# A recurrent layer on one core: q normalised channel-major by two broadcast rows instead of token-major per chunk

## The reference

```python
q = hidden_states @ Wq
k = hidden_states @ Wk
v = hidden_states @ Wv
beta = jax.nn.sigmoid(hidden_states @ Wb + bb)
q = silu(causal_dwconv(q, qconv_w, qconv_b))      # 4 taps along the tokens
k = silu(causal_dwconv(k, kconv_w, kconv_b))
q = layernorm(q.reshape(Bs, Ls, H, DK), qn_w, qn_b)   # over the 128 channels of a head
k = layernorm(k.reshape(Bs, Ls, H, DK), kn_w, kn_b)
...
def step(S, inp):
    q_t, k_t, v_t, b_t = inp
    b = b_t[..., None, None]
    S = (1.0 - b) * S + b * (v_t[..., :, None] * k_t[..., None, :])
    o_t = jnp.einsum('bhvk,bhk->bhv', S, q_t)
```

## Time and profile before

| what | before |
|---|---|
| median of 3 runs (lowest, highest) | 2654.92 us (2653.37, 2655.7) |
| profiled execution, its own time | 2649.24 us |
| its span, first to last instruction | 2647.5 us |
| busy share of the span: PE / PEld / DVE / ACT / POOL | 96% / 85% / 67% / 42% / 32% |
| mean granted TensorE clock, share of full speed | 0.987 |

### The profile page before, as it was taken

The page is one execution under the profiler, slowest core; times in us unless marked ns, Lnnn a source line. Parts: engine busy times, 40 slices in busy tenths (PEclk is TensorE's granted clock), DMA queues, the critical chain, the costliest instruction groups (busy, mean ns, idle before and its releaser), DMA issues. The chain is left out here.

```text
span 2647.5 us, 44202 instructions
## 1 busy us (share of the span) xinstructions
PE 2538.9 (96%) x15744; PEld 2254.0 (85%) x15744; DVE 1779.9 (67%) x3716; ACT 1122.9 (42%) x1513; POOL 849.7 (32%) x442
## 2 busy tenths in 40 slices
PE   5899999999999999999999999997899999999997
PEld 4789889999999989999998999997788887888886
DVE  5678888888888888888888888888431222433232
ACT  5444454444444444444444444444432323322221
POOL 1245445443434334343434334344100000211220
PEclk8999999999999999999999999999999999999998
DMA  7544443643333353333354333342461101441320
GB/s 273 167 136 153 151 135 128 219 133 104 119 119 119 111 176 125 119 127 104 118 169 134 119 108 122 119 128 80 156 230 49 63 32 56 128 150 48 111 84 27
DMA packets 220876, 327.51 MB, mean 124 GB/s; under 512 B 56310, under 2 KB 156918, under 8 KB 216058
## 3 DMA queue, kind: packets, MB, share of 16 engines
q1 hardware_dynamic: 125946, 192.21, 22.2%
q10 hardware_dynamic: 86144, 109.06, 12.4%
q0 software_dynamic: 8704, 25.19, 3.1%
HBM read 237.77 MB, written 97.03 MB: 126 GB/s over the span
## 5 line engine op out<-in xcount | busy, mean ns | idle before, releaser
L983 DVE SCALAR_TENSOR_TENSOR xn_rows<-ps_proj,conv,xn_rows 128x1021 f32<-128x1021 f32 x381 | 488.0, 1281 | 127.8 <-ACT xn_rows L890 118.7
L1160 PE MATMUL ps_proj<-xt_hi,w_hi 128*128 128x512 f32 x1008 | 411.7, 408 | 20.1 <-DVE xn_rows L983 13.6
L1162 PE MATMUL ps_proj<-xt_hi,w_lo 128*128 128x512 f32 x1008 | 396.8, 394 | 0.0
L1161 PE MATMUL ps_proj<-xt_lo,w_hi 128*128 128x512 f32 x1008 | 395.4, 392 | 0.0
L941 ACT ACTIVATE rc_tok_k<-rc_tok_k,rc_small 128x128 f32<-128x128 f32 x512 | 204.2, 481 | 353.2 <-DVE rc_small L1017 353.2
L782 POOL TENSOR_TENSOR rc_k_state<-rc_tok_k,k_norm_rows 128x1024 f32<-128x1024 f32 x64 | 153.5, 2399 | 515.1 <-issue 397.5
L1182 PE MATMUL ps_proj<-wv_hi,xt_hi 128*128 128x256 f32 x1024 | 294.9, 288 | 0.6 <-PEq L75 0.6
L1183 PE MATMUL ps_proj<-wv_lo,xt_hi 128*128 128x256 f32 x1024 | 289.5, 283 | 0.0
L1184 PE MATMUL ps_proj<-wv_hi,xt_lo 128*128 128x256 f32 x1024 | 289.3, 283 | 0.0
L814 POOL TENSOR_TENSOR rc_small<-rc_small,rc_minus_half 128x16 f32<-128x16 f32 x64 | 187.2, 2924 | 218.9 <-DVE rc_small L1012 218.9
L890 ACT ACTIVATE xn_rows<-ps_proj,conv 128x1024 f32<-128x1024 f32 x127 | 152.9, 1204 | 231.7 <-PE rc_ps_work L1136 231.7
(11 more groups left out here) (177 smaller groups left out, 5770.9 us busy)
## 6 DMA issues: line engine op xcount, KB each, us to landing
rc_decay_all<-scratch_decay ACTq DMA_DIRECT2D x64, 512.0 KB, 3.5
rc_cum_all<-scratch_cum ACTq DMA_DIRECT2D x64, 512.0 KB, 3.6
scratch_o<-rc_o_sb ACTq DMA_DIRECT2D x64, 512.0 KB, 3.2
w_hi<-scratch_w_split SPq DMA_DIRECT2D x48, 512.0 KB, 4.0
w_lo<-scratch_w_split SPq DMA_DIRECT2D x48, 512.0 KB, 4.8
wv_hi<-scratch_wv_split SPq DMA_DIRECT2D x24, 512.0 KB, 3.9
wv_lo<-scratch_wv_split SPq DMA_DIRECT2D x24, 512.0 KB, 4.8
scratch_w_split<-w_hi SPq DMA_DIRECT2D x16, 512.0 KB, 2.8
```

Source lines behind the costliest of these rows:

```text
L983: nc.vector.scalar_tensor_tensor(out=act_cm[j][:, back:], in0=projected[:, 0:L - back], scalar=conv[par][:, j, t:t + 1], in1=act_cm[j][:, ...
L1160: nc.tensor.matmul(out, hi, xt_hi[:, k, cols], start=k == 0, stop=False)
L1161: nc.tensor.matmul(out, hi, xt_lo[:, k, cols], start=False, stop=False)
L1162: last = nc.tensor.matmul(out, lo, xt_hi[:, k, cols], start=False, stop=k == KC - 1)
```

## The change

**q's way.** The turned q is not copied out of PSUM any more and not turned back. ACT writes silu of q into a tile of its own (`q_silu`, two buffers). PE turns it only for its statistics, which DVE now takes straight from PSUM (`statistics(0)` reads `work(QT)`). The reciprocal standard deviation and the shift go into one small tile `rstd_shift` (128 tokens of a chunk as partitions; for q 16 columns: 8 chunks of rstd, 8 of shift). After the projection of v PE turns these 16 columns in one product into a 16 x 128 block of PSUM. ACT copies the block to `q_row_parts` and stores it to DRAM as 16 pieces of 512 bytes (`store_rows`), which lie there as two rows of 1024 values. Then, behind the normalising of k, ACT issues a load of the two rows to all 128 partitions (`load_rows`, `q_rows`, 128 x 2048 f32). In the next step DVE multiplies the channel-major q by the first row and adds the second, in place (`scale_q`: two tensor-tensor instructions of 128 x 1024, right behind the scan), and ACT reads that tile for `q_cm`.

**What goes with it.** On ACT `store_rows` stands before the normalising of k and waits for PE's product; `load_rows` stands behind it, before the eviction of the outputs. On DVE `normalise` and its 8 instructions are gone, and `statistics(0)` stands before `convolve(0)`. The turn of q before the projection of k is one instead of two. `ps_work` has six uses a step, so the waits on it are others: the turn of k waits until the statistics of q have read PSUM, the turn back of k until the outputs of the head before have been evicted. POOL's power waits for the product of the head before. `w_raw` and `wv_raw` now lie in tiles that the later stages use. A few semaphores are merged in `stage_tokens` and in the ranking, with the same order as before.

```diff
@@ pool
-                    nc.gpsimd.tensor_tensor(small[:, 6], small[:, 5], minus_half[:], ALU.pow
+                    after_step(pool, "q_rows_turned", B_.i - 1)
+                    nc.gpsimd.tensor_tensor(rstd_shift[:, :, 0], small[:, 5], minus_half[:], ALU.pow
                                             ).then_inc(S["rstd_done"], 1)
@@ act
-                def tokens(j):
...
+                def store_rows():
+
+                    after_step(act, "q_rows_turned", B_.i)
+                    after_step(act, "q_rows_stored", B_.i - 1, 16)
+                    nc.scalar.activation(q_row_parts[:], work(SC)[0:2 * NC, 0:P], ACT.Copy
+                                         ).then_inc(S["q_rows_copied"], 1)
+                    after_step(act, "q_rows_copied", B_.i)
+                    act.dma_start(row(scratch["q_rows"], B_.i).rearrange("(m p) -> m p", p=P), q_row_parts[:]
+                                  ).then_inc(S["q_rows_stored"], 16)
+
+                def load_rows():
+
+                    after_step(act, "q_rows_stored", B_.i, 16)
+                    after_step(act, "q_scaled", B_.i - 1, 2)
+                    act.dma_start(q_rows[:].rearrange("p k t -> p (k t)"),
+                                  row(scratch["q_rows"], B_.i).partition_broadcast(P)
+                                  ).then_inc(S["q_rows_loaded"], 16)
...
                 if C_.live:
-                    ready(0, "q_back", "q_ready", q_cm[C_.par])
+                    ready(0, "q_scaled", 2, q_silu[C_.par][:], "q_ready", q_cm[C_.par])
                 if B_.live:
                     load_decay(B_.par, B_.i, B_.pair)
-                    tokens(0)
...
                 if B_.live:
-
+                    store_rows()
                     after_step(act, "rstd_done", B_.i)
                     after_step(act, "shift_done", B_.i)
                     for c in range(NC):
...
                     last.then_inc(S["k_normed"], 1)
+                    load_rows()
@@ dve
-                def normalise():
-                    after_step(dve, "shift_done", B_.i)
-                    for c in range(NC):
-                        last = nc.vector.tensor_scalar(tok[0][:, c], tok[0][:, c], small[:, 6, 0, c:c + 1],
-                                                       small[:, 7, 0, c:c + 1], ALU.mult, ALU.add)
-                    last.then_inc(S["q_normed"], 1)
+                def scale_q():
+
+                    after_step(dve, "q_rows_loaded", C_.i, 16)
+                    after_step(dve, "q_turned", C_.i)
+                    nc.vector.tensor_tensor(q_silu[C_.par][:], q_silu[C_.par][:], q_rows[:, 0], ALU.mult
+                                            ).then_inc(S["q_scaled"], 1)
+                    after_step(dve, "q_scaled", C_.i, 2, 1)
+                    nc.vector.tensor_tensor(q_silu[C_.par][:], q_silu[C_.par][:], q_rows[:, 1], ALU.add
+                                            ).then_inc(S["q_scaled"], 1)
...
                                                  ALU.mult, ALU.add).then_inc(S["dmat_done"], 1)
+                    scale_q()
+                if B_.live:
+                    statistics(0)
                 if A_.live and not first_done(A_.i):
                     convolve(0)
                 if B_.live:
-                    statistics(0)
                     statistics(1)
...
-                if B_.live:
-                    normalise()
@@ pe
-                if C_.live:
-                    after_step(pe, "q_normed", C_.i)
-                    after_step(pe, "scores_done", D_.i - 1)
-                    turn(work(par, QB), lambda c: tok[0][:, c]).then_inc(S["q_back"], 1)
...
                 if B_.live:
                     after_step(pe, "k_silu", B_.i)
-                    after_step(pe, "q_tok", B_.i)
-                    turn(work(par, KT), lambda c: act_cm[1][:, c * P:(c + 1) * P]).then_inc(S["k_turned"], 1)
+                    after_step(pe, "stats_done", B_.i, 2, 1)
+                    turn(work(KT), lambda c: act_cm[1][:, c * P:(c + 1) * P]).then_inc(S["k_turned"], 1)
...
+                if B_.live:
+
+                    after_step(pe, "rstd_done", B_.i)
+                    after_step(pe, "shift_done", B_.i)
+                    if D_.live:
+                        after_step(pe, "scores_done", D_.i)
+                    nc.tensor.transpose(work(SC)[0:2 * NC, 0:P], rstd_shift[:, 0].rearrange("p k c -> p (k c)"),
+                                        ident[:]).then_inc(S["q_rows_turned"], 1)
                 if D_.live:
 
                     after_step(pe, "states_done", D_.i, NC - 1)
```

More of the change, by code:

```diff
@@ L538, in stage_recurrence @@
         act_cm = [keep["xn_rows"][:].rearrange("p t d -> p (t d)")[:, j * L:(j + 1) * L] for j in range(2)]
-        tok = [sb("tok_q", [P, NC, P]), sb("tok_k", [P, NC, P])]
+        tok_k = sb("tok_k", [P, NC, P])
+        q_silu = two("q_silu", [P, L])
+        q_rows = sb("q_rows", [P, 2, L])
         q_cm = two("q_cm", [P, L])
@@ L595, in stage_recurrence @@
         VC = NC // 2
-        QB, QT, KB, KT, UP, SC, OUT = range(7)
+        QT, KB, KT, UP, SC, OUT = range(6)
         class At:
@@ L879, in ready @@
                         after_step(act, "q_cum_done", C_.i - 2)
-                    nc.scalar.activation(out[:], work(par, (QB, KB)[j]), ACT.Identity,
+                    nc.scalar.activation(out[:], source, ACT.Identity,
                                          bias=norm[:, j, 1:2], scale=norm[:, j, 0:1]).then_inc(S[name_out], 1)
@@ L904, in silu @@
                     after_step(act, n + "_conv", B_.i, PAD)
-                    nc.scalar.activation(act_cm[j], act_cm[j], ACT.Silu).then_inc(S[n + "_silu"], 1)
+                    if j == 0:
+                        after_step(act, "q_turned", B_.i - 2)
+                        after_step(act, "q_ready", B_.i - 2)
+                    nc.scalar.activation((q_silu[B_.par][:], act_cm[1])[j], act_cm[j], ACT.Silu
+                                         ).then_inc(S[n + "_silu"], 1)
                 if B_.live:
@@ L1766, in build @@
             keep["beta_steps"] = first_stages.enter_context(nc.sbuf_tensor("beta_steps", [P, s.NC, s.N], F32))
-            for part, dt in (("w_raw", F32), ("w_hi", F32R), ("w_lo", F32R)):
-                keep[part] = [first_stages.enter_context(nc.sbuf_tensor(f"{part}{i}", [P, 2, s.KC, P], dt))
-                              for i in range(2)]
-                keep["wv" + part[1:]] = first_stages.enter_context(nc.sbuf_tensor("wv" + part[1:], [P, s.KC, 2 * P], dt))
+            for part in ("hi", "lo"):
+                keep["w_" + part] = [first_stages.enter_context(nc.sbuf_tensor(f"w_{part}{i}", [P, 2, s.KC, P], F32R))
+                                     for i in range(2)]
+                keep["wv_" + part] = first_stages.enter_context(nc.sbuf_tensor("wv_" + part, [P, s.KC, 2 * P], F32R))
+            keep["w_raw"] = [keep["raw"][:, i * s.L:(i + 1) * s.L].rearrange("p (j k n) -> p j k n", j=2, k=s.KC)
+                             for i in range(2)]
+            keep["wv_raw"] = kept.x_rows[:].rearrange("p t d -> p (t d)")[:, 0:2 * s.L // 2].rearrange(
+                "p (k n) -> p k n", k=s.KC)
             taps = a["qconv_w"].shape[1]
```

111 lines of the change are left out of this document (57 added, 54 removed).

## The result

The changed kernel is slower: 2725.06 us (median of 4 runs, 2717.41 to 2726.54) against 2655.31 us (median of 4 runs, three at 2653.37 to 2655.70 and one at 3346.36), a ratio of 1.0263 with a 95% interval of 1.0244 to 1.0283. The forecast was 2635 us with a range of 2605 to 2690.

What follows compares the result with a forecast made beforehand. PE bounds the kernel at 26.97 us a step; DVE would at 26.5. 46 steps gain 21.6, 15 x 0.3 adds 4.5, less 6 gives 20 us: 2629 profiled, 2635 us as median, range 2605 to 2690.

Steps and rivals of the forecast that it cites:

- PE's own step: On PE, the removed turn of q less the added 16-column product: 26.97 us a step becomes 26.24.
- The collision: In `scale_q` on DVE, POOL's weighting takes the port between product and sum, 2.3 us; 4.7 us in all with rows in time.
- DVE's round: DVE's work per step with rows in time: 26.05 us even, 26.75 odd, mean 26.4, replacing PE as bound by a hair.
- the first rival: PE keeps the bound at 26.24 us a step, by early rows or fewer collisions: 2617 us, without any collision 2607; chance 0.22.
- reading PSUM costs DVE more: Statistics of q on DVE: taken at the SBUF price, 1.65 us for eight; the skill's rule would add some 0.5 us.
- The store of the rows: ACT's small store of the rows to DRAM, taken to land after 1.9 us, as the smallest store in the table.
- late again and again: Rows' load lands about 5.5 us after issue, or its issue does not run ahead: 27.35 us mean step, 2692 us; chance 0.20.
- The load of 1 MB: ACT's load of the two rows to all partitions: 4.8 us taken, 3.5 to 6.1, issued at 1036.9, landing at 1041.7.
- A late step: On DVE, POOL's weighting goes first: 7.3 us behind the scan, 2.6 more; one step in four or five, next in time.
- First sequence: Steps where POOL also splits weights: 0.3 us gain in each of 15 steps, 4.5 us together.
- Drain: At the kernel's end nothing hides the rows' way: a loss of 4 to 8 us, taken as 6.

Runs made afterwards that it cites:

- the run with all three edits: Changed kernel with POOL's weighting released by the second half of `scale_q`, 50 waits at the head of DVE's program, and `wv` loads behind the rows: 2624.16 us.
- the run with the moved loop: Changed kernel with 50 waits on a value long reached put in front of DVE's second loop, so that its body lies 50 instructions later: 2707.12 us.
- with the rows early: Changed kernel with 50 waits before DVE's second loop and the rows' load ahead of their store, reading the rows of the step before: 2628.38 us.

## Why the prediction was wrong

**PE's own step.** 26.24 us was predicted; 26.23 is what every run shows in which DVE is quick enough. The product of 16 columns takes 0.27 us, and the outputs start 0.11 behind it. (From 599.75 to the drain the trace of before has 45 steps, two of them longer, where the prediction counts 46; that is 0.5 us in its sum.)

**The collision.** Predicted: 2.3 us of POOL's weighting between the two instructions. Over all 64 steps (groups by line: count, us in all, mean ns, idle before):

```profile
L1052 DVE TENSOR_TENSOR rc_q_silu<-rc_q_silu,rc_q_rows 128x1024 f32<-128x1024 f32 x64 | 210.9, 3296 | 2.2
L1016 DVE BATCH_NORM_STATS2 rc_stats<-rc_ps_work 128x6 f32<-128x128 f32 x512 | 106.9, 277 | 2.7 <-PE rc_ps_work L1161 2.7
L1016 DVE BATCH_NORM_STATS2 rc_stats<-rc_tok_k 128x6 f32<-128x128 f32 x512 | 104.7, 277 | 11.3 <-ACT rc_tok_k L903 11.2
```

The sum takes 3296 ns where it takes 1225 alone: 2.1 us, where 2.3 were foreseen from the earlier trace rows. DVE's round with the rows in time is 25.5 and 26.3 us (26.05 and 26.75 predicted), so PE stays the bound there: the first rival was nearer than the forecast. The rule of the Trainium skill (SBUF — State Buffer, section Who interferes with whom), that such a pair does not run side by side, held in every step: none of the 64 sums took less than 3.2 us. The other one (VectorE: DVE Perf Modes, section The TRN2 errata), that reading PSUM costs DVE more, does not show here: 277 ns for a statistic from either place, as the forecast took it.

**The store of the rows: the step that failed first.** The prediction took 1.9 us for it from the earlier trace rows. In half of the steps of the loop it is 1.4, in the other half 3.6 to 4.0. The rival "late again and again" looked at the `wv` loads and put them aside as issued 4 us before the load of the rows. That is right, and it overlooks that the load waits for the store, that the `wv` loads are issued beside the store, since the end of the projection of v lets both go, and that they hold it up. The load of 1 MB was taken right for the steps without `wv` alone. Its median is 4.8 us in the run with all three edits (first line) and 5.1 with DVE's loop written out (second line; DMA issues: KB, median us to landing):

```profile
rc_q_rows<-scratch_q_rows ACTq DMA_DIRECT2D x64, 1024.0 KB, 4.8
...
rc_q_rows<-scratch_q_rows ACTq DMA_DIRECT2D x64, 1024.0 KB, 5.1
```

In the loop of the second run it is 4.7 us behind a quick store and 5.6 behind a slow one. (The changed kernel has no landings of this load; its late products start 5.9 us behind the issue in the median.) By the prediction's own terms a store of 3.7 us, issued at 1033.9, lets the load go out at 1037.6 instead of 1036.9 and puts the rows at 1042.4, with a load of 5.6 us at 1043.2: behind the scan in either kind of step (1041.1 and 1041.8). That is the rival of the other side, at both of its points, the landing of "about 5.5 us" and the "issue that does not run ahead". Its price was summed too low: with 2.6 us more in an even step its own rounds are 28.65 and 26.75, 27.7 in the mean and not 27.35, which makes some 2708 us instead of 2692; the run with the moved loop, late rows and no fetch in its 44 steps took 2707.12. (In a step without `wv` the load goes out 1.4 us behind the store, not 3.0 as summed: the queue runs further ahead of the normalising than the 0.7 us taken.) A late step in the loop of the changed kernel mostly costs DVE 2.5 us, near the 2.6 predicted: it stands 1.2 to 2.0 us, and the slow product takes the rest. The prediction put off a late step by saying that the next one makes up for it. With a round of 25.9 us in the mean and PE at 26.23 DVE makes up 0.3 us a step, not 2.6: one late step in two makes DVE the bound for good. Taking the lateness away is worth 64 us with the loop moved (2707.12 to 2642.92) and 62 at the old place (2725.06 to 2663.33), where the gaps became shorter, too.

**The turn of DVE's loop: the cause that no rival had.** The edit made DVE's program shorter (counted in the two programs, the second loop begins at its instruction 791 instead of 833 and is 301 long instead of 311), and in its new place instructions are fetched at each turn. `normalise`, which stood behind the last wait of the body, went, too. Moving the loop is worth 18 to 20 us beside the collision (2725.06 to 2707.12, 2663.33 to 2642.92), and 42 without it (2669.49 to 2627.63). The order of the instructions does not show the fetch; the trace of before had the same wait once, at the single turn of the loop in the first sequence, and the prediction did not ask what it was:

```profile
305.46 1.22 DVE L1033 TENSOR_TENSOR rc_v_beta<-ps_proj,beta_steps 128x1024 f32<-128x1024 f32 x1 [3.81 <-issue]
```

**The ends.** First sequence: 4.5 us of gain predicted, 16.4 of loss measured; with the rows early it is 415.4 against 415.2. That run still has the fetch at the loop's turn (33.8 us against 31.2) and the step in which DVE runs the 50 waits (32.4 against 27.4); its other 13 steps gain 7.3 us together. So the gain is there, and the late rows and the fetch outweigh it. Drain: 6 predicted, 9.1 measured.

The sum with both causes taken away, 2642.92 us, lies 8 us from the forecast of 2635: 44 steps at 26.23 instead of 26.5 gain 12, the first sequence (429.4) and the drain lose more than that. So the nearness is in part luck. The terms for PE, for the collision and for a load alone were about right, but even then it is the first rival that holds in the loop, PE at 26.23 us, and not a DVE round of 26.4. What the sum left out were two things beside its path: what else the end of the projection of v releases when it starts the small store, and where the loop comes to lie.

## What to carry to other kernels

Before a small transfer is put on the path, list what other queues the same semaphore releases: 8 KB beside 1 MB took 3.6 to 4.0 us instead of 1.4, and one more wait in front of the big load gave 62 us back. When an edit changes the length of an engine's program, look in the trace for waits on "issue" at the turn of its loops and for packets of the instruction queue in steady state; 50 idle instructions ahead of the loop were enough to be rid of them. An engine whose own round is within 1.3% of the bound (25.9 of 26.23 us) cannot make up for 2.5 us that are lost in every second step, and a collision that is harmless by itself can raise a delay of 1.2 us to that.

## What the runs showed of the hardware that was not expected

Whether a loop of VectorE is fetched anew depends on where it lies: the same 301 instructions, 50 further on, took no packet instead of 5 of 8 KB for each turn. 208 waits on a value long reached are not free either: they held DVE for 19.3 us, 0.09 us each.

A gap of PE of some 3 us can be followed by a stretch at half its clock. PE's busy time, granted clock (1.00 is 2.4 GHz, 0.5 is 1.2), DMA share and GB/s in stretches of the changed kernel around one turn:

```profile
1092.00:1104.80 12.80, 10.11 (x66) 1.00 0.66 208
1104.80:1105.80 1.00, 0.99 (x4) 1.00 0.00 0
1105.80:1109.20 3.40, 3.40 (x9) 0.51 0.00 0
1109.20:1123.00 13.80, 13.80 (x106) 1.00 0.44 153
```

PE stands 2.7 us before 1104.81, starts again at full clock, and 1 us later runs 3.4 us at half. This follows six of the ten turns. Here it costs nothing, since DVE is the bound: this step is 31.1 us long (1092.22 to 1123.35), and the four turns at which the clock stays at 1.00 take 31.1 to 31.3. At two of those four PE had stood 2.7 and 2.8 us as well.
